# Softmax weights in a Trainium2 decoder layer: GpSimd's scaling pass folded into ScalarE and VectorE, and made a step earlier in the first group

## The reference

```
h = layernorm(x)
q = h @ Wq.T ;  kc = h @ Wk_down.T ; vc = h @ Wv_down.T
k, v = halves of concat(kc, vc per head) @ Wk_up.T, Wv_up.T
scores = where(causal, q k^T / sqrt(128), -1e9)
attn   = softmax(scores)                # the softmax weights
x      = x + (attn @ v) @ Wo.T
```

## Time and profile before

| | us |
|---|---|
| median of 3 runs | 1096.59 (1095.89 to 1096.82) |
| the profiled execution | 1095.9 |
| its span, first to last instruction | 1094.1 |
| PE busy | 1064.7 (97%) |
| DVE busy | 905.0 (83%) |
| ACT busy | 531.4 (49%) |
| POOL busy | 407.3 (37%), of it 198.6 in line 782 |

### The profile page before, as it was taken

How to read it: one execution, slowest core, us unless ns; L and a number is a source line. 1 busy time by engine, 2 the same in 40 slices (tenths; PEclk the granted TensorE clock), 3 DMA queues, 4 the chain that set the end, 5 groups by cost and what they waited for, 6 DMA issues and landing times.

```text
span 1094.1 us, 19695 instructions
## 1 busy us (share of the span) xinstructions
PE 1064.7 (97%) x6257; PEld 568.5 (52%) x6257; DVE 905.0 (83%) x1862; ACT 531.4 (49%) x1082; POOL 407.3 (37%) x423
## 2 busy tenths in 40 slices
PE   6999988999999999999999999999999999999998
PEld 5976544555555555555555555555555554444443
DVE  7979588988787978887888888888878799889973
ACT  5665366555454445454545444544545455143430
POOL 2239655544343434353533434344425233000000
PEclk9999999999999999999999999999999999999999
DMA  8026146654554445455544454455455378404442
GB/s 320 11 94 228 65 90 156 148 127 114 130 125 115 108 116 138 111 120 140 134 107 121 127 119 105 119 134 132 105 125 128 84 161 234 154 15 93 96 107 87
DMA packets 227489, 135.21 MB, mean 124 GB/s; under 512 B 198000, under 2 KB 200176, under 8 KB 226544
## 3 DMA queue, kind: packets, MB, share of 16 engines
q1 hardware_dynamic: 227440, 134.59, 48.6%
HBM read 68.23 MB, written 17.83 MB: 79 GB/s over the span
## 4 chain that ended last, share of the span: by engine, by line
PE 82%; DVE 11%; ACT 3%; issue 2%; DMA 1%; POOL 1%; DVEq 0%; POOLq 0%; ACTq 0%; SPq 0%
PE ps L1781 79%; ACT prob L1057 1%; DVE prob L1471 1%; PE ps L2040 1%; DVE wo_sb L1232 1%; DVE h_b L1232 1%; PE ps L1801 1%; DVE x_sb L1648 1%; DMA wq_sb<-wo_in 1%; DVE prob_t L1232 1%; DVE x_sb L1453 1%; DVE x_sb L1634 0%; DVE stats L1240 0%; DVE prob_s L1232 0%; DVE stats L1651 0%
## 5 line engine op out<-in xcount | busy, mean ns | idle before, releaser
L782 POOL TENSOR_SCALAR prob<-prob,row_inv 128x128 f32<-128x128 f32 (+3 forms) x256 | 198.6, 795 | 441.3 <-DVE row_inv L1442 441.3
L1781 PE MATMUL ps<-wo_sb,o_t 128*128 128x512 f16 x1536 | 351.7, 379 | 1.8 <-DVE x_sb L1453 1.7
L1781 PE MATMUL ps<-h_b,wq_sb 128*128 128x512 f16 x1524 | 343.2, 380 | 0.0
L1057 ACT ACTIVATE prob<-prob,neg_max 128x128 f32<-128x128 f32 (+3 forms) x256 | 140.6, 550 | 224.2 <-DVE neg_max L1477 224.2
L1781 PEld LDWEIGHTS ps<-h_b,wq_sb 128*128 128x128 f16 x1524 | 147.9, 98 | 176.4 <-issue 1.4
L1781 PEld LDWEIGHTS ps<-wo_sb,o_t 128*128 128x128 f16 x1536 | 147.1, 98 | 170.5 <-DVE x_sb L1453 5.7
L1453 DVE SCALAR_TENSOR_TENSOR x_sb<-ps,x_sb 128x512 f32<-128x512 f32 x256 | 174.3, 685 | 51.5 <-PE ps L1781 50.5
L1781 PE MATMUL ps<-prob_t,v_sb 128*128 128x128 f16 (+2 forms) x960 | 115.9, 273 | 7.0 <-DMA prob_t<-prob_s 7.0
L1781 PE MATMUL ps<-k_t,q_t 128*128 128x512 f16 (+3 forms) x768 | 114.8, 299 | 0.4 <-DVE neg_max L1477 0.3
L1471 DVE CUSTOM_DVE_ANT_0 prob<-ps,mask 128x512 f32<-128x512 f32 (+3 forms) x256 | 110.2, 484 | 2.3 <-issue 1.6
L1781 PEld LDWEIGHTS ps<-prob_t,v_sb 128*128 128x128 f16 x960 | 83.2, 98 | 36.9 <-DMA prob_t<-prob_s 7.9
(11 more groups left out here) (151 smaller groups left out, 1145.8 us busy)
## 6 DMA issues: line engine op xcount, KB each, us to landing
wq_in<-in_wq SPq DMA_DIRECT2D x64, 256.0 KB, 3.4
wo_in<-in_wo SPq DMA_DIRECT2D x32, 512.0 KB, 3.9
side_in<-in_ctx SPq DMA_DIRECT2D x16, 512.0 KB, 4.4
kv_parts<-wo_sb SPq DMA_DIRECT2D x7, 1024.0 KB, 5.5
x_sb<-in_x SPq DMA_DIRECT2D x8, 512.0 KB, 10.0
ctx_quantised<-side_out SPq DMA_DIRECT2D x16, 256.0 KB, 3.0
h_b<-ctx_quantised SPq DMA_DIRECT2D x2, 2048.0 KB, 10.7
out<-x_sb SPq DMA_DIRECT2D x8, 512.0 KB, 3.0
```

Source lines behind the costliest of these rows:

```text
L782: ins = nc.gpsimd.tensor_scalar(at, at, row_inv[:, u % 2, q:q + 1], S_P, ALU.mult, ALU.mult)
L1057: ins = nc.scalar.activation(at, at, ACT.Exp, bias=neg_max[:, n % 2, q:q + 1], scale=SOFTMAX, accum_out=row_sum[:, n % 2, q:q + 1])
L1781: ins = nc.tensor.matmul(out_, lhs(i), rhs(j), start=start and n == 0, stop=stop and n == 3 * len(pairs) - 1)
```

## The change

GpSimd's pass at line 782 is removed, with its semaphore. In its place:

- `inverses` on VectorE is two instructions: the reciprocal, then, after a wait for it, a multiplication of the 128x4 inverses by S_P.
- `p_split` on ScalarE is four activations, one for each query tile, each with its own column of `row_inv` as scale, where it was one copy of 1280 columns. It waits for `inv_done` instead of `prob_normed`.
- `p_split` on VectorE is four scalar_tensor_tensor that multiply by the same column and subtract the high part, where it was one.
- In the first group, both `p_split(u)` stand in step u, behind `o_split(u-2)`, for u = 0 to 6. In all other groups, and for unit 7 of the first, they stay where they were, a step later.

```
@@ gpsimd, group @@
-                    pool.wait_ge(inv_done, UNITS * g + u + 1)
-                    pool.sem_inc(pool_passed)
-                    for q in range(QT):
-                        at = prob[:, u % 2, S_AT[q]:S_AT[q] + (q + 1) * P]
-                        ins = nc.gpsimd.tensor_scalar(at, at, row_inv[:, u % 2, q:q + 1], S_P, ALU.mult, ALU.mult)
-                    ins.then_inc(prob_normed, 1)
@@ scalar, p_split @@
-                act.wait_ge(prob_normed, UNITS * g + n + 1)
+                act.wait_ge(inv_done, UNITS * g + n + 1)
...
-                split_hi(prob_s[:, 0, :], prob[:, n % 2, :], p_hi, 1.0)
+                for q in range(QT):
+                    at = slice(S_AT[q], S_AT[q] + (q + 1) * P)
+                    ins = nc.scalar.activation(prob_s[:, 0, at], prob[:, n % 2, at], ACT.Identity,
+                                               scale=row_inv[:, n % 2, q:q + 1])
+                ins.then_inc(p_hi, 1)
@@ scalar, group @@
-                    if not (first and u == 0):
+                    if not first:
                         p_split(g, u - 1)
                     exponentials(g, u)
                     if not (first and u < LAG):
                         o_split(g, u - LAG)
+                    if first and u < UNITS - 1:
+                        p_split(g, u)
@@ vector, inverses and p_split @@
-                nc.vector.reciprocal(row_inv[:, n % 2, :], row_sum[:, n % 2, :]).then_inc(inv_done, 1)
+                nc.vector.reciprocal(row_inv[:, n % 2, :], row_sum[:, n % 2, :]).then_inc(inv_raw, 1)
+                dve.wait_ge(inv_raw, UNITS * g + n + 1)
+                nc.vector.tensor_scalar(row_inv[:, n % 2, :], row_inv[:, n % 2, :], S_P, None, ALU.mult)\
+                    .then_inc(inv_done, 1)
...
-                split_lo(prob_s[:, 1, :], prob[:, n % 2, :], prob_s[:, 0, :], p_lo, 1.0)
+                for q in range(QT):
+                    at = slice(S_AT[q], S_AT[q] + (q + 1) * P)
+                    ins = nc.vector.scalar_tensor_tensor(prob_s[:, 1, at], prob[:, n % 2, at], row_inv[:, n % 2, q:q + 1],
+                                                         prob_s[:, 0, at], ALU.mult, ALU.subtract)
+                ins.then_inc(p_lo, 1)
```

More of the change, by code:

```diff
@@ L341, in decoder_layer @@
         pow_done = sem("pow_done")
-        prob_normed = sem("prob_normed")
+        inv_raw = sem("inv_raw")
         var_done = sem("var_done")
```

## The result

The changed kernel takes 1115.09 us (median of 4 runs, 1114.18 to 1118.1), the one before on the same chip 1096.24: a ratio of 1.0183 [1.0171, 1.0195], or 18.9 us slower. The forecast was 1115.4. The profiled execution has a span of 1113.5 us against 1094.1.

What follows compares the result with a forecast made beforehand. TensorE was taken to bound the middle groups, with VectorE nearly level in the first. First group 18.3 us plus last group 0.5 on 1095.9 gave 1114.7, 1115.4 against the median; 8-in-10 range 1107 to 1126.

Steps and rivals of the forecast that it cites:

- The serial part: First group, each step: from the maxima to the block's split 8.54 us instead of 5.36, 3.18 more.
- its 1112 us: Whole-kernel time if three extra split instructions cost 0.18 and 0.28 us by the skill page, not 0.45 and 0.67.
- The six steps: First group, VectorE from unit 0's maxima to unit 6's: about 74 us instead of 57.19.
- The 3 us taken off for GpSimd: First group: GpSimd's additions come mostly while VectorE waits, 3 us less; bounds 3.3 off and 3.4 on.
- The end of the group: First group, from unit 6's maxima to its end: 21.6 us instead of 20.2, 1.4 more.
- the wait that I named: Step 6, first group: TensorE's fourth chunk waits for an addition behind the low part, 9.2 us after the maxima.
- The middle groups: Six groups after the first: splits cost VectorE 5.3 us a group against 16.1 free, costed at nothing.
- rival 1: Middle groups, steps 3 and 7: late additions hold TensorE 0.5 us each, 7 us on top, 1122 us; chance 0.14.
- The last group: Last group: the last unit's longer low part lies on the path where VectorE is late, 0.5 us more.
- rival 2: First group: TensorE's new waits bring slow spells; at 1.2 GHz throughout, 4.9 us more in six steps, 1145 us; chance 0.05.
- rival 3: First group: TensorE's transpose waits and slow spell vanish, VectorE's idle time is covered, 8.7 us less, 1088 us; chance 0.07.
- rival 4: First group: what early transposes win pays for the longer steps, no effect, 1097 us; chance 0.04.

Runs made afterwards that it cites:

- the run with spare matmuls: The changed kernel plus matmuls, their result never read, in TensorE's waits of the first group: 1116.34 us, 1.0194 of the kernel before.
- the fold with sums held: The changed kernel with splits a step later in every group, GpSimd's sums waiting for VectorE's query splits and context rounding: 1098.86 us.
- three units moved: The changed kernel with only units 0 to 2 of the first group split in their own step, later ones a step later: 1105.64 us.
- one instruction each: The changed kernel with both splits as one instruction over 1280 columns and no scaling by the inverse row sums: 1108.86 us.

## Why the prediction was right

- **The serial part.** Worked out: 8.54 us; measured: 8.51. Its terms: the second `row_inv` instruction 0.21, as forecast; ScalarE's four activations 1.92 for 1.93; VectorE's four 1.86 from start to start (159.98 to 161.84), as forecast. Against the one-piece splits that is 0.66 us more on ScalarE and 0.45 on VectorE. Not all of it is the price of three more instructions: each piece also takes its scale from a column. With the same 512 columns from SBUF, 128 to 230 us of the changed kernel:

```profile
L812 ACT ACTIVATE wq_sb<-wq_in 128x512 f16<-128x512 f32 x12 | 7.2, 614 | 0.0
L1046 ACT ACTIVATE prob_s<-prob,row_inv 128x512 f16<-128x512 f32 x7 | 4.9, 706 | 0.0
L1487 DVE SCALAR_TENSOR_TENSOR prob_s<-prob,row_inv,prob_s 128x512 f16<-128x512 f32 x7 | 5.2, 747 | 0.0
```

  The column adds 92 ns a piece on ScalarE and, against the 685 ns of `wq_sb<-q_tmp`, 62 on VectorE. Four times that taken off leaves some 0.29 and 0.20 us for three instructions, an estimate from these rows. The prediction weighed 0.28 and 0.18 for them from the Trainium skill ("Perfetto Trace Analysis", section "Optimizing Scalar/DVE Operations"). The trace agrees with that; what its 1112 us left out is the column.
- **The six steps.** 74.1 against 73.7 us. Steps 0 and 1 grew by 6.9 for 7.2, steps 2 to 5 by 9.6 for 9.7. The 3 us taken off for GpSimd came out: against 3.18 a step, steps 2 and 3 are 1.5 and 0.9 short, and steps 4 and 5 0.35 each (there `b_out` took 0.99 us before and takes 0.68, `wo_sb` 1.35 behind a wait of 0.18 and now 1.22), 3.1 in all. But it was a guess of when GpSimd's sums would start, and one collision was only moved: `q_t` in step 3 now takes 2.46 us beside the sum of the context, where a block's split took 2.38.
- **The end of the group.** 22.35 us from unit 6's maxima (204.98) to the next group, for 21.6 forecast. The size is near, but what the profiled execution shows is not the wait that I named. TensorE waits for the split of `wo_sb` and then does step 6 without a wait, its first two chunks in a low-clock spell (5.28 us for 12 matmuls). It comes to the third chunk only at 213.70 and to the fourth six matmuls later, when the addition that this one needs is done (214.34):

```profile
201.84 1.22 DVE L1232 SCALAR_TENSOR_TENSOR wo_sb<-wo_in,wo_sb 128x1024 f16<-128x1024 f32 x1
...
203.17 5.28 PE L1790 MATMUL ps<-wo_sb,o_t 128*128 128x512 f16 x12 [3.63 <-issue]
...
213.65 0.69 DVE L1456 SCALAR_TENSOR_TENSOR x_sb<-ps,x_sb 128x512 f32<-128x512 f32 x1
213.70 2.75 PE L1790 MATMUL ps<-wo_sb,o_t 128*128 128x512 f16 x12
```

  In the run with spare matmuls the first two chunks take 2.75 us, and the forecast wait stands in the open, ahead of the fourth chunk and with step 7 behind it:

```profile
212.33 1.94 DVE L1487 SCALAR_TENSOR_TENSOR prob_s<-prob,row_inv,prob_s 128x128 f16<-128x128 f32 x4 [1.20 <-ACT prob_s L1046]
214.19 0.68 DVE L1456 SCALAR_TENSOR_TENSOR x_sb<-ps,x_sb 128x512 f32<-128x512 f32 x1
...
214.93 1.47 PE L1790 MATMUL ps<-wo_sb,o_t 128*128 128x512 f16 x6 [2.48 <-DVE x_sb L1456]
```

  So both ways end within 0.3 us of one another after unit 6's maxima (22.6 there), and that is why the faster clock won nothing at this place.
- **The middle groups**, costed at nothing, take 1.74 us more: a quarter of rival 1's 7 us. Waits there were also named as a sign of being wrong, and two appear, 0.4 us in all. But VectorE's longer step 7 is not the cause, though a sum of GpSimd lengthens its rounding there, in the second group of the changed kernel:

```profile
329.14 1.92 POOL L741 TENSOR_TENSOR wq_in<-q_tmp,wq_in 128x512 f32<-128x512 f32 x1 [8.80 <-DVE wq_sb L1232]
```
```profile
329.85 1.76 DVE L1601 TENSOR_SCALAR side_out<-side_in 128x1024 bf16<-128x1024 f32 x1
```

  Before, the pass kept this sum behind the rounding, which then took 1.10 us. Even so the last split of step 7 starts 3.21 us after the next group's first scores (334.38 against 331.17), and 3.48 us after them before (317.42 against 313.94). What grew is the turn of VectorE's loop over the middle groups. Its first instruction after it, before, in the changed kernel, and in the fold with sums held:

```profile
318.02 0.68 DVE L1471 CUSTOM_DVE_ANT_0 prob<-ps,mask 128x512 f32<-128x512 f32 x1
```
```profile
338.03 0.69 DVE L1474 CUSTOM_DVE_ANT_0 prob<-ps,mask 128x512 f32<-128x512 f32 x1 [2.97 <-issue]
```
```profile
317.03 0.69 DVE L1480 CUSTOM_DVE_ANT_0 prob<-ps,mask 128x512 f32<-128x512 f32 x1 [3.27 <-issue]
```

  Every kernel without the pass has 2.2 to 3.3 us of such idle time at each of the five turns (the loop runs six groups), and the kernels with the pass none. With the sums held ScalarE's half of the last split comes later, 2.78 us after the first scores (312.41) for 1.69 (332.86), and so does the turn. The first maxima of a group so start 4.08 us after its first scores with the pass, 6.1 to 6.9 without, and 6.9 to 7.4 with the sums held in all groups. All that a middle group loses is lost in its step 0, and it is what goes beyond some 6.2 us: nothing at 6.12, 0.65 us at 6.86, 1.20 at 7.40. With three units moved the five turns lie at 6.08 to 6.34, and the middle groups take 623.2 us. In the same kernels, and in no others, one queue of instruction loads has about twice the packets; before and changed, by their profiles (packets, MB, share):

```profile
q14 instruction: 22, 0.18, 0.1%
```
```profile
q14 instruction: 47, 0.39, 0.1%
```

  From 331 to 852 us the changed kernel loads five or six packets a group there, the kernel before one in all in its last five middle groups. So VectorE's loop, longer by the fold, seems to be loaded again at each turn. The kernel with one instruction each has the same turns and ScalarE's list at its old length, which points to VectorE's. How long the loop may be was not tried.
- **The last group**: 0.5 us forecast, 0.4 measured behind it and nothing in it. The start's 1.4 us less lies in unchanged code and nearly offsets the misses of the end and the middle: that the medians come within 0.3 us of the forecast is in part luck, while the first group, 18.6 us for 18.3, is not.
- **The rivals.** The clock (rival 2) had its spells, 17 us of them, and the run with spare matmuls shows that they cost nothing. The faster case (rival 3) needed VectorE's step within 8.6 us; the shortest is 10.32; "no effect" (rival 4) needed 9.5. That early transposes were worth having was true as far as it went: TensorE's waits for them are gone in the changed kernel, but VectorE sets the pace.

## What to carry to other kernels

An engine that fills its wait for another with work of the step before loses that cover when the work is moved into the same step: price the move as the serial chain between the two engines, once a step, not as the work that it shifts. A wait on TensorE that looks like the loss may be slack of another engine's bound; what pays is what shortens that engine's step, here keeping GpSimd's sums off VectorE's splits in the one stretch where VectorE sets the pace. The same hold costs time where it makes the sums late for their reader, so a hold is to be placed by stretch. And instructions added to a loop are to be priced at its turn too: look for idle time there and for packets on the instruction queues.

## What the runs showed of the hardware

- GpSimd's four-part pass takes 2.06 or 2.07 us while VectorE waits and 2.5 to 4.0 us in the first group before, where VectorE works beside it.
- A `neg_max` of four columns takes 0.17 us alone and 1.23 behind a GpSimd sum that had started 0.06 us earlier.
- A rounding of 1024 columns on VectorE takes 0.69 us alone and 1.76 us behind a GpSimd sum; a split's `q_t` part goes to 2.46 us behind one that had just begun.
- Low-clock spells of 3.4 to 10.2 us came and went with the filling of TensorE's waits, and the time of the group moved by at most 1.3 us, most of which was that `neg_max`.
- A scale taken from a column makes a ScalarE activation of 512 columns 92 ns longer (706 for 614) and a VectorE split 62 ns (747 for 685).
- VectorE idles 2.2 to 3.3 us at each turn of its loop where the instruction queue has 46 or 47 packets, and not where it has 22.
